# Moving the first row load, the blanking and the weight split in the two attention stages of a two-layer transformer kernel

## The reference

```python
x = L0_attn_x
xn = _layernorm(x, axis=-1)
x = x + _L0_attn_ref(xn, ...) + _L0_ffn_ref(xn, ...)
xn = _layernorm(x, axis=-1)
x = x + _L1_attn_ref(xn, ...) + _L1_ffn_ref(xn, ...)
```

## Time and profile before

| | us |
|---|---|
| median of 3 runs | 2241.44 |
| the runs | 2241.33 to 2242.36 |
| the profiled execution, its own time | 2235.95 |
| its span | 2234.3 |
| PE busy in the span | 1764.3 (79%) |
| DVE busy | 1122.0 (50%) |
| ACT busy | 1024.8 (46%) |
| POOL busy | 1012.5 (45%) |

### The profile page before, as it was taken

How to read it: one execution, slowest core, us unless ns; L and a number is a source line. 1 busy time by engine, 2 the same in 40 slices (tenths; PEclk the granted TensorE clock), 3 DMA queues, 4 the chain that set the end, 5 groups by cost and what they waited for, 6 DMA issues and landing times. The chain is left out here.

```text
span 2234.3 us, 33907 instructions
## 1 busy us (share of the span) xinstructions
PE 1764.3 (79%) x10759; PEld 1101.2 (49%) x10759; DVE 1122.0 (50%) x2399; ACT 1024.8 (46%) x1356; POOL 1012.5 (45%) x778
## 2 busy tenths in 40 slices
PE   3888889870599999999999638887887888747933
PEld 2455555540387787787787523333433433235510
DVE  3666666537513313313313148878787787437211
ACT  1455555543313322222223117877787788813400
POOL 3344444320234344343333407777777677724212
PEclk8899999985799999999999858989998999869965
DMA  3333333306201101101100253222222222043999
GB/s 102 87 96 94 94 104 91 94 11 202 84 1 47 47 0 47 47 0 47 45 2 28 77 174 86 67 71 80 80 66 71 81 65 59 10 173 137 345 318 330
DMA packets 129732, 204.38 MB, mean 91 GB/s; under 512 B 14303, under 2 KB 84063, under 8 KB 129668
## 3 DMA queue, kind: packets, MB, share of 16 engines
q1 hardware_dynamic: 107896, 163.40, 24.6%
q10 hardware_dynamic: 16096, 20.65, 2.6%
q0 software_dynamic: 5680, 19.57, 2.2%
HBM read 95.96 MB, written 56.69 MB: 68 GB/s over the span
## 5 line engine op out<-in xcount | busy, mean ns | idle before, releaser
L761 POOL TENSOR_TENSOR l_prob<-l_prob,l_bias 128x1024 f32<-128x1024 f32 x192 | 452.1, 2375 | 149.2 <-ACT l_prob L865 148.4
L1315 POOL TENSOR_TENSOR f_hl<-f_full,f_hh 128x512 fp32r<-128x512 f32 x192 | 247.6, 1290 | 439.9 <-DVE f_hh L1357 283.2
L922 DVE CUSTOM_DVE_ANT_0 l_slot<-l_slot,l_bias 128x512 f32<-128x512 f32 x512 | 340.4, 714 | 52.8 <-PE l_slot L999 51.7
L1357 DVE CAST f_hh<-f_full 128x512 fp32r<-128x512 f32 x128 | 74.8, 585 | 397.7 <-ACT f_full L1336 396.2
L868 ACT ACTIVATE l_prob<-l_prob 128x1024 f32<-128x1024 f32 x256 | 271.1, 1071 | 0.0
L1401 PE MATMUL f_ps<-f_hh,f_hi_h 128*128 128x512 f32 x1024 | 267.1, 397 | 0.0
L1411 PE MATMUL f_ps<-f_hl,f_hi_h 128*128 128x512 f32 x1024 | 265.8, 396 | 0.0
L429 DVE TENSOR_REDUCE l_peak<-l_slot 128x2 f32<-128x256 f32 (+3 forms) x256 | 206.2, 821 | 111.3 <-PE l_slot L526 109.0
L1336 ACT ACTIVATE f_full<-f_ps,f_h_s 128x512 f32<-128x512 f32 x128 | 86.3, 687 | 332.6 <-PE f_ps L1411 308.9
L372 ACT ACTIVATE l_prob<-l_slot 128x1024 f32<-128x1024 f32 (+3 forms) x256 | 174.7, 706 | 96.3 <-PE l_slot L545 93.4
L1401 PEld LDWEIGHTS f_ps<-f_hh,f_hi_h 128*128 128x128 f32 x1024 | 192.8, 188 | 49.3 <-ACT f_hh L1329 2.7
(11 more groups left out here) (209 smaller groups left out, 2691.5 us busy)
## 6 DMA issues: line engine op xcount, KB each, us to landing
l_stacks<-l_parts SPq DMA_DIRECT2D x384, 128.0 KB, 2.7
inter<-e_stage POOLq DMA_DIRECT2D x32, 512.0 KB, 5.1
c_rows<-inter SPq DMA_DIRECT2D x32, 512.0 KB, 9.6
attn<-l_out_sb ACTq DMA_DIRECT2D x16, 512.0 KB, 2.8
f_raw<-in_L_ffn_h_w SPq DMA_DIRECT2D x16, 512.0 KB, 4.2
e_w<-in_L_ffn_f SPq DMA_DIRECT2D x32, 256.0 KB, 4.4
l_bias<-ext ACTq DMA_DIRECT2D x16, 448.0 KB, 11.8
l_x_in<-in_L_attn_x SPq DMA_DIRECT2D x8, 512.0 KB, 3.8
```

The source lines that it names most:

```text
L761: return eng.tensor_tensor(probs(n), src, bias[:, h:h + 2, j * P:j * P + T], ALU.add)
L922: ins = dve.tensor_tensor_reduce(src, src, bias[:, 4 * g + 2 * pr + a, t * P:t * P + T], 1.0, 3 * NEG, ALU.add, ALU.max, peak[:, g, a, pr, ...
L1315: pool.tensor_tensor(hl[layer % 2][:, o], full[:, n % 2], hh[layer % 2][:, o].bitcast(F32), ALU.subtract).then_inc(h_lo.sem, 1)
```

## The change

Both attentions get a helper `opening(b)`, true for batch 0 alone where its number is a constant, and with it:

1. SP issues the load of `x_in` for batch 0 ahead of all constants and weights, no longer as the first event of turn -1; the other batches keep their event. Of the constants, `power` is loaded before `ident`.
2. POOL blanks `stacks[:, 1]`, DVE blanks `stacks[:, 0]`; `blank.sem` is waited for at 3.
3. DVE's split of the low parts moves from its entry to the event behind the last `ln` of batch 0 (layer 0) or behind `shift` of batch 0 (layer 1). In layer 1 ACT's high parts move behind `ln` of batch 0 as well; in layer 0 they stay at ACT's entry.
4. In layer 1 POOL no longer waits for the bias tables at its entry: before its first `prob` event of each group of heads in batch 0 it waits for that group's tables.

`low_weights` holds the splits as they stood at DVE's entry, six in layer 0 and four in layer 1.

```diff
 # layer 0 (layer 1 alike, with "ident", "power" and "wo" alone)
-                    if kind == "x_load":
+                    if kind == "x_load" and not opening(b):
                         wait(sp, xn_ready, TT, b - 1)
...
-                for dst, src in ((ident, c["c_ident"]), (power, c["c_pow"]), (cols, c["c_cols"]), (half, c["c_half"])):
+                sp.dma_start(x_in[:], x_d[0].rearrange("(t p) d -> p t d", p=P)).then_inc(x_loaded.sem, 16)
+                for dst, src in ((power, c["c_pow"]), (ident, c["c_ident"]), (cols, c["c_cols"]), (half, c["c_half"])):
...
-                sp.wait_ge(blank.sem, 2)
+                sp.wait_ge(blank.sem, 3)
...
-                pool.memset(stacks[:].bitcast(F32), 0.0).then_inc(blank.sem, 1)
+                pool.memset(stacks[:, 1].bitcast(F32), 0.0).then_inc(blank.sem, 1)
...
                     if kind == "ln":
...
+                        if n == TT - 1 and opening(b):
+                            low_weights()
...
+                dve.memset(stacks[:, 0].bitcast(F32), 0.0).then_inc(blank.sem, 1)
                 turns(dve, emit)
 # layer 1
                     if kind == "prob" and pooled(n):
+                        if n % 8 == 0 and opening(b):
+                            pool.wait_ge(bias_in[n // 8].sem, 16 * 4)
                         wait(pool, p_copied, added(n)[1], b)
...
                 pool.wait_ge(consts_in.sem, 16 * 3)
-                for g in range(QUADS):
-                    pool.wait_ge(bias_in[g].sem, 16 * 4)
                 turns(pool, emit)
...
+                def high_weights():
+                    for name, dst in (("q", wq), ("k", wk), ("v", wv)):
+                        act.wait_ge(w_in[name].sem, 16)
+                        act.activation(dst[:, 0], raw[name], ACT.Copy, scale=HD ** -0.5 if name == "k" else 1.0)\
+                           .then_inc(w_high.sem, 1)
+                    act.wait_ge(consts_in.sem, 16 * 3)
+                    act.copy(wo[:, 0], raw["o"]).then_inc(w_high.sem, 1)
...
                                            scale=rstd[:, t:t + 1]).then_inc(xn_ready.sem, 1)
+                        if opening(b):
+                            high_weights()
...
                            .then_inc(shift_ready.sem, 1)
+                        if opening(b):
+                            low_weights()
```

More of the change, by code:

```diff
@@ L234, in turns, with opening @@
             turn(B)
+        def opening(b):
+            return isinstance(b, int) and b == 0
         def wait(eng, tally, k, b):
@@ L394, in _, with low_weights @@
             def _(dve):
+                def low_weights():
+                    dve.wait_ge(w_high.sem, 2)
+                    for twice in range(2):
+                        cut = slice(twice * LATENT, (twice + 1) * LATENT)
+                        dve.tensor_tensor(wc[:, 1, :, cut], raw["c"][:, :, 0:LATENT], wc[:, 0, :, cut].bitcast(F32),
+                                          ALU.subtract).then_inc(w_ready.sem, 1)
+                    dve.wait_ge(w_high.sem, 3)
+                    dve.tensor_tensor(wq[:, 1], raw["q"][:], wq[:, 0].bitcast(F32), ALU.subtract).then_inc(w_ready.sem, 1)
+                    dve.wait_ge(w_high.sem, 4)
+                    dve.scalar_tensor_tensor(wk[:, 1], raw["k"][:, 0], HD ** -0.5, wk[:, 0].bitcast(F32),
+                                             ALU.mult, ALU.subtract).then_inc(w_ready.sem, 1)
+                    dve.wait_ge(w_high.sem, 5)
+                    dve.tensor_tensor(wv[:, 1], raw["v"][:, 0], wv[:, 0].bitcast(F32), ALU.subtract).then_inc(w_ready.sem, 1)
+                    dve.wait_ge(w_high.sem, 6)
+                    dve.tensor_tensor(wo[:, 1], raw_wo[:], wo[:, 0].bitcast(F32), ALU.subtract).then_inc(w_ready.sem, 1)
                 def emit(kind, b, n, i):
@@ L793, in emit @@
                               .then_inc(tops_in[n].sem, 16)
-                for dst, src in ((ident, c["c_ident"]), (power, c["c_pow"])):
+                sp.dma_start(x_in[:], x_d[0].rearrange("(t p) d -> p t d", p=P)).then_inc(x_loaded.sem, 16)
+                for dst, src in ((power, c["c_pow"]), (ident, c["c_ident"])):
                     sp.dma_start(dst[:], src).then_inc(consts_in.sem, 16)
@@ L888, in _, with low_weights @@
             def _(dve):
+                def low_weights():
+                    for m, (name, dst) in enumerate((("q", wq), ("k", wk), ("v", wv), ("o", wo))):
+                        dve.wait_ge(w_high.sem, m + 1)
+                        dve.scalar_tensor_tensor(dst[:, 1], raw[name], HD ** -0.5 if name == "k" else 1.0,
+                                                 dst[:, 0].bitcast(F32), ALU.mult, ALU.subtract).then_inc(w_ready.sem, 1)
                 def emit(kind, b, n, i):
```

## The result

| | us |
|---|---|
| median of 6 runs, kernel before | 2241.39 (2237.09 to 2246.76) |
| median of 6 runs, changed kernel | 2228.24 (2224.04 to 2232.58) |
| ratio | 0.9942, 95% interval 0.9925 to 0.9959 |
| profiled execution, its own time | 2224.04 (before 2235.95) |
| its span | 2222.4 (before 2234.3) |

The change made the kernel faster, by 13 us in this comparison, where 8.5 us were forecast. The median lies 0.3 us under the low end of the range.

A forecast was written before the change was run, and what follows sets the result against it. PE waits at each attention's start for a chain from the `x_in` load to the transposes. Gains of 5.9 us in layer 0 and 2.6 in layer 1 sum to 8.5: 2241.44 - 8.5 = 2232.9, range 2228.5 to 2237.5.

The forecast's parts named there:

- Layer 0's sum, 5.9 us: Start of layer 0: PE's first transposes at 14.75 instead of 20.67 us, 5.9 us gained.
- bound of 11.0: Layer 0: latest landing of `wo` if `x_in` does not fit beside the other loads; gain then 4.6 us.
- Layer 1's sum, 2.6 us: Start of layer 1: transposes at 1300.9 instead of 1303.49, 2.6 us gained; bounds 1.0 and 5.6.
- I take 1294.0: Layer 1: assumed landing of `wo` behind `x_in` on SP's queue, between 1291.0 and 1295.6.
- The second term: Layer 1: high parts 2.5 us, last low part 0.73, then 0.14 before PE, now behind the rows.
- the second rival: Layer 1: `x_in` slips into the idle start, `wo` lands at 1291; 11.5 us gained, 2229.9; chance 0.14.
- so I add 1.5 us to each side: Whole kernel: range widened by 1.5 us each side, as the granted clock's changes need not move with the work.
- The 5.5 us between the profiled execution and the median: Kernel before: median 5.5 us above the profiled execution's 2235.95, unexplained and taken to stay.
- Exclusion of the memsets: Layer 0: DVE's memset begins only after POOL's two; total gain 4.7 us, 2236.7; chance 0.04.
- Nothing in layer 1: Layer 1: `wo` lands at 1296.6 or later, splits eat the earlier `rstd`; 5.9 us total, 2235.5; chance 0.15.
- Slower by the clock: First turns of layer 0: full clock granted later relative to PE's work; 2246; chance 0.03.
- The old distance of 22.3 us: Layer 0: first scores should follow the transposes by 22.3 us as before; otherwise the prediction is wrong.

The follow-up runs named there:

- layer 0's part alone: Layer 0's attention as changed, layer 1's as before, against the kernel before: ratio 0.9972 (0.9956 to 0.9987), 6.3 us.
- part 4 undone: Changed kernel, but POOL waits for all bias tables at layer 1's entry again: transposes 33.3 us behind the block's start; executed once, its time not read.
- the waits by use: Changed kernel with `power` and `ident` on their own semaphore and weights awaited at first use: ratio 0.9908 to the kernel before, median 2218.0.
- three traces: Whole change unchanged, profiled in the first comparison and two repeats: ratios to the kernel before 0.9942, 0.9947 and 0.9961.
- 23 and 45 runs: All runs of the changed kernel and the kernel before over three comparisons: means 2228.8 and 2239.3 us.
- idle matmuls: Changed kernel plus matmuls on blanked values at PE's entry, 28 in layer 0 and 56 in layer 1: ratio 0.9961 to the kernel before, median 2231.46.
- 20 matmuls: Changed kernel with weights awaited at first use, tables on SP's queue, 20 idle matmuls in layer 0, 22 in layer 1: ratio 0.9869, median 2212.23.

## Why the prediction was right or wrong

**Layer 0's sum, 5.9 us.** Right in what follows what, and 14.85 against 14.75 in the end, with two small errors that nearly cancel: `wo` landed at 9.97 and not at 9.65 (no backlog worth the bound of 11.0), and from the rows' end at 12.47 to the transposes it took 2.4 us and not 2.65. DVE's memset cost 3.47 us (3.6 expected) but began at 3.25 and not at 2.46, so the statistics came at 6.64 and not at 6.1, hidden behind `wo`. The runs of layer 0's part alone gave 6.3 us.

**What holds what.** Right in both layers: `rstd` waits for `wo`, PE for the last split, and the tables are off the path only because of part 4. The runs with part 4 undone (33.3 us; my 33.5) and with the waits by use bear it out from both sides.

**Layer 1's sum, 2.6 us: the term that was mis-sized.** The step reads "I take 1294.0" for the landing of `wo`, 21.1 us behind the block's start, so `rstd` at 21.3; it began at 19.6, 19.3 and 19.4 in the three traces. I carried over that SP's queue moves one packet for each of the tables' all along. It does so later, but in the first six microseconds it moved 0.54 MB where it had moved 0.28, as rows of 1 KB took the turns of the constants' small ones and the tables gave way. Of the 5.75 us that could have been added, 2.4 were, where I took 4.2. The second term, the splits behind the rows, cost 3.15 us and not 3.37, because ACT begins a high part every 0.52 us though each lasts 0.61: 0.2 us. Together they are the 2.1 us between 2.6 and 4.7. The truth lay between the forecast and the second rival, but not by the way that this rival names: the room was not idle, both queues together moved 1.35 MB in those six microseconds and 1.42 before.

**The range.** The sum of the rows as measured is 10.6 us, and the means of 23 and 45 runs differ by 10.5; my 8.5 is 2 us short of it. With the landing of `wo` right, the forecast would have been about 2230.8 and the measured 2228.24 well inside a range as wide as mine. The first comparison's 13 us lies another 2.5 us beyond the rows, and against that the step "so I add 1.5 us to each side" was too narrow. I read the spread of the kernel from three runs that happened to lie within 1.0 us; 45 runs spread over 16 us. The 5.5 us between the profiled execution and the median, which I did not explain, lie within that spread too. Executions with the same layer 0 entered layer 1's block 5 us apart (1272.9 and 1278.0; 1266.1 and 1271.6). Their granted clocks differ: in the changed kernel's first six runs the lowest time had a mean of 0.901 and the highest 0.892. A median of six inherits one or two microseconds of that (an estimate from the spread of the 23 and 45 runs), on both sides of the ratio.

**The rivals.** Exclusion of the memsets: refuted, 3.47 us beside POOL's 3.50. Nothing in layer 1: refuted, it gives 5.8 us alone. Slower by the clock: no comparison shows it; the clock moves single executions both ways, and its mean over the runs is 0.896 before and after. From the transposes to the first score of layer 1 the traces of the changed kernel took 19.0, 20.7 and 20.2 us, at a granted clock of 0.78, 0.69 and 0.69. The rule of the Trainium skill on the start (TensorE: Matmul & The Clock Gate, Part 1: The HAM clock gate), that the number of slow matmuls differs between runs of one kernel, agrees.

**"The old distance of 22.3 us"** from transposes to first score in layer 0 was 22.8, 21.9 and 23.0: not wrong, but a mark finer than the executions' own difference.

## What to carry to other kernels

A counting semaphore that gathers several loads makes each waiter wait for the last of them: here a 2 KB constant was counted with the last weight, and giving it a count of its own, with the weights awaited at their first use, brought another 9 to 10 us, nearly as much as the whole change. When a load is moved to the front of a queue that shares the transfer engines with another, ask in bytes what it delays in the first microseconds, where the steady ratio of packets need not hold and where small rows may be taking the turns. And take the spread of a kernel from enough runs before setting a range: three that agree say little.

## What the runs showed of the hardware

- A four-element DVE instruction waited for a POOL memset. With POOL blanking all of `stacks`, DVE's `TENSOR_SCALAR` of 128x4 began at 6.15 us and lasted 5.18 instead of 0.17, until 11.33; POOL's memset ended at 11.30. In layer 1 of the same kernel it happened again: 2.66 us, until 1282.77, under a memset that ended at 1282.74. DVE's statistics (4.43 to 5.84) and its own memset (3.25 to 6.72 in the changed kernel) ran beside POOL's memsets at their usual length, and in the kernel before so did the splits of `wc`, with two inputs each (0.49 us for the two, from 10.26 on the earlier trace rows; 0.48 in the changed kernel). In layer 0 that cost little, since POOL, which makes `rstd`, was busy until then itself (11.48 against 11.30); where the next step is another engine's, it could cost the whole wait, which no run here shows. The Trainium skill (SBUF — State Buffer, Who interferes with whom) has `tensor_scalar` among the instructions that may take the ports shared with GpSimd, with the second comer blocked for the whole length of the first; both rows agree. I had weighed the rule for the memset alone, where it did not apply, and not for the small instruction behind it, where it did.
- A 512 KB load took 3.9 us from issue to landing in layer 0, 6.3 beside the tables on ACT's queue, 18.9 behind the weights on the same queue and beside the tables, and 3.8 with tables and weights behind it on its own queue.
- After 14.8 us of idle matmuls PE was at full clock, and 10.9 us of standstill later at half again, with 0.60 on average from 1290 to 1296. After 3.5 us of standstill (layer 0, 28 matmuls) the transposes ran at 0.50; after 2.6 us (layer 0, 20 matmuls) and 1.7 us (layer 1, 22 matmuls) they ran at full, but after 2.7 us more the projections of layer 1 were at 0.50.
